# Attention and feed-forward on one core: the output of each head scaled and added on VectorE in place of ScalarE and GpSimd

## The reference

```
xn  = layernorm(x)                       # x: 2048 x 256
q,k,v = projections of xn                # 16 heads of width 128
p   = softmax(causal_mask(k q) / sqrt(128))
out = sum over heads of (p v) W_O        # 2048 x 256
y   = x + out + W2 . fwht(silu(W1 xn) * (W3 xn))
```

## Time and profile before

| | |
|---|---|
| median of 3 runs | 1452.96 us (1447.12 to 1454.21) |
| the profiled execution, its own time | 1451.85 us |
| its span, first to last instruction | 1450.0 us |
| granted TensorE clock, mean | 0.98 |
| attention stage, 16 periods | from about 286 us to about 1410 us |
| GpSimd's adds L369 | 128 of 1293 ns, 165.4 us in all |
| ScalarE's scalings L570 | 256 of 490 ns, 109.4 us in all |

### The profile page before, as it was taken

One profiled execution on the slowest core, in us unless ns is written; L12 is line 12 of the kernel. 1 busy time (PEld: TensorE's weight loads), 2 busy tenths in 40 slices (PEclk: granted clock), 3 DMA queues, 4 the chain that ended last, 5 costly groups with the idle time before them and its releaser, 6 DMA issues.

```text
span 1450.0 us, 26628 instructions
## 1 busy us (share of the span) xinstructions
PE 1351.6 (93%) x8104; PEld 1195.5 (82%) x8104; DVE 957.7 (66%) x2133; ACT 931.0 (64%) x1879; POOL 996.1 (69%) x660
## 2 busy tenths in 40 slices
PE   3989999969999999999999999999999999999985
PEld 2778888758888888888888888888888888888875
DVE  7743300277777777777777777777777767777760
ACT  3312244457777777777777777777777777777772
POOL 4420000066979797979797979797979787979785
PEclk8999999989999999999999999999999999999998
DMA  4100056579898989898988898888888888888884
GB/s 147 69 1 0 0 145 186 169 228 286 248 281 259 288 256 286 270 286 253 285 263 280 259 289 268 284 259 280 255 281 270 265 275 266 284 269 288 248 266 153
DMA packets 278459, 335.14 MB, mean 231 GB/s; under 512 B 62736, under 2 KB 251280, under 8 KB 273808
## 3 DMA queue, kind: packets, MB, share of 16 engines
q1 hardware_dynamic: 278416, 334.65, 73.6%
HBM read 173.08 MB, written 161.48 MB: 231 GB/s over the span
## 4 chain that ended last, share of the span: by engine, by line
PE 36%; POOL 23%; issue 20%; DVE 7%; ACT 5%; DMA 4%; SPq 3%; POOLq 0%; DVEq 0%; ACTq 0%
POOL pt_lo L378 15%; PE ps L827 12%; PE ps L828 12%; PE ps L829 12%; POOL acc L369 5%; SPq L276 3%; DMA scratch<-raw 3%; ACT raw L546 2%; DVE had L759 2%; DVE raw L769 2%; POOL v_lo L383 1%; DVE k_lo L672 1%; ACT pt_hi L555 1%; DMA raw<-w3t 1%; DMA pt_lo<-scratch 1%
## 5 line engine op out<-in xcount | busy, mean ns | idle before, releaser
L378 POOL TENSOR_TENSOR pt_lo<-pt_lo,pt_hi 128x640 fp32r<-128x640 f32 (+11 forms) x384 | 661.8, 1753 | 161.2 <-ACT pt_hi L555 161.1
L546 ACT ACTIVATE raw<-ps,had 128x1024 f32<-128x1024 f32 (+7 forms) x384 | 329.5, 867 | 226.0 <-DVE had L762 206.5
L769 DVE STREAM_TRANSPOSE raw<-raw 128x2048 f32<-128x2048 f32 (+15 forms) x256 | 322.0, 1292 | 99.5 <-ACT raw L546 97.2
L827 PE MATMUL ps<-pt_hi,v_hi 128*128 128x256 f32 (+1 forms) x1152 | 326.8, 284 | 29.7 <-POOL pt_lo L378 29.2
L828 PE MATMUL ps<-pt_lo,v_hi 128*128 128x256 f32 (+1 forms) x1152 | 331.7, 288 | 0.0
L829 PE MATMUL ps<-pt_hi,v_lo 128*128 128x256 f32 (+1 forms) x1152 | 329.8, 286 | 0.0
L555 ACT CAST pt_hi<-pt_lo 128x640 fp32r<-128x640 f32 (+11 forms) x384 | 283.4, 819 | 15.1 <-DMA pt_lo<-scratch 14.9
L759 DVE TENSOR_REDUCE had<-ps 128x1 f32<-128x1024 f32 (+1 forms) x256 | 238.0, 950 | 64.7 <-PE ps L829 64.5
L827 PEld LDWEIGHTS ps<-pt_hi,v_hi 128*128 128x128 f32 x1152 | 222.2, 193 | 38.6 <-issue 30.1
L827 PE MATMUL ps<-k_hi,q_hi 128*128 128x512 f32 (+3 forms) x640 | 239.0, 373 | 7.4 <-ACT raw L546 7.4
L829 PE MATMUL ps<-k_hi,q_lo 128*128 128x512 f32 (+3 forms) x640 | 234.6, 366 | 0.0
(11 more groups left out here) (102 smaller groups left out, 2218.3 us busy)
## 6 DMA issues: line engine op xcount, KB each, us to landing
all_values<-raw SPq DMA_DIRECT2D x16, 1024.0 KB, 5.0
v_next<-all_values SPq DMA_DIRECT2D x16, 1024.0 KB, 5.4
scratch<-raw SPq DMA_DIRECT2D x64, 256.0 KB, 5.5
pt_lo<-scratch SPq DMA_DIRECT2D x16, 1024.0 KB, 5.4
scratch<-raw SPq DMA_DIRECT2D x64, 240.0 KB, 5.0
pt_lo<-scratch SPq DMA_DIRECT2D x16, 960.0 KB, 6.0
scratch<-raw SPq DMA_DIRECT2D x64, 224.0 KB, 5.2
pt_lo<-scratch SPq DMA_DIRECT2D x16, 896.0 KB, 4.8
```

Of the source, the lines that this page charges most:

```text
L378: pool.tensor_tensor(lo, lo.bitcast(F32), hi.bitcast(F32), ALU.subtract).then_inc(pt_lo_done, 1)
L546: act.activation(to[:, first // P:(first + n) // P], ps[:, a * BANK:a * BANK + n].rearrange("p (i g k) -> p i g k", g=4, k=BLK), ACT.Exp, ...
L769: dve.transpose(v, v).then_inc(blocked, 1)
L827: pe.matmul(dst, a[0], b[0], start=start, stop=False, skip_group_check=True)
```

## The change

`output` moves from ScalarE to VectorE, where it is one SCALAR_TENSOR_TENSOR for each 128 queries: ring bank times `row_rcp` plus `acc`, written to `acc`. GpSimd's `add` and the two `share` buffers go. VectorE's new `output` stands in every step, behind `z_to_lo` of the small chunk and ahead of `maxima`; in step s it takes the chunk whose product TensorE made in step s-1. The ring bank is now free when VectorE has added it.

```diff
@@ gpsimd
-            def add(h, z):
-                c = Z_ORDER[z]
-                pool.wait_ge(shared, z_count(h, z))
-                pool.tensor_tensor(acc[:, 2 * c:2 * c + 2, :], share[:, z % 2, :, :],
-                                   acc[:, 2 * c:2 * c + 2, :], ALU.add).then_inc(out_added, 1)
...
-                        if not (first and back) and not (over and not back):
-                            add(h + back, z)
@@ scalar
-            def output(h, z):
-                c = Z_ORDER[z]
-                act.wait_ge(rcp_done, z_count(h, z))
-                wait(act, out_added, z_count(h, z) - 2)
-                act.wait_ge(wo_product, z_count(h, z))
-                for t in range(2):
-                    j = 2 * c + t
-                    ins = act.activation(share[:, z % 2, t, :], ring_bank(("O", z))[:, t * D:(t + 1) * D], ACT.Copy,
-                                         scale=row_rcp[:, j:j + 1])
-                ins.then_inc(shared, 1)
...
@@ vector
+            def output(h, z):
+
+                c = Z_ORDER[z]
+                dve.wait_ge(rcp_done, z_count(h, z))
+                dve.wait_ge(wo_product, z_count(h, z))
+
+                wait(dve, out_added, z_count(h, z) - 1)
+                for t in range(2):
+                    j = 2 * c + t
+                    ins = dve.scalar_tensor_tensor(
+                        out=acc[:, j, :], in0=ring_bank(("O", z))[:, t * D:(t + 1) * D], scalar=row_rcp[:, j:j + 1],
+                        in1=acc[:, j, :], op0=ALU.mult, op1=ALU.add)
+                ins.then_inc(out_added, 1)
...
-                for s in range(5 if over else STEPS):
+                for s in range(6 if over else STEPS):
                     if s in O_SMALL and not absent(O_SMALL[s][0]):
                         z_to_lo(h + O_SMALL[s][0], O_SMALL[s][1])
+
+                    back, z = (O_SMALL if s % 2 else O_BIG)[(s - 1) % STEPS]
+                    if s == 0:
+                        back -= 1
+                    if not absent(back):
+                        output(h + back, z)
                     if not over:
                         maxima(h, s, 0)
                         maxima(h, s, 1)
@@ tensor, ring_wait
-                    pe.wait_ge(shared, z_count(h - back - (1 if i >= 3 else 0), i))
+                    pe.wait_ge(out_added, z_count(h - back - (1 if i >= 3 else 0), i))
```

More of the change, by code:

```diff
@@ L127, in attention_ffn_kernel @@
         aux = sb("aux", [P, 4 * BANK], F32)
-        share = aux[:, 0:2 * BANK].rearrange("p (b t d) -> p b t d", b=2, t=2)
         mask = aux[:, 2 * BANK:3 * BANK]
@@ L212, in attention_ffn_kernel @@
         wo_product, rcp_done, summed = sem("wo_product"), sem("rcp_done"), sem("summed")
-        shared, out_added = sem("shared"), sem("out_added")
+        out_added = sem("out_added")
         G_FREE = 2
@@ L407, in period @@
                             p_to_lo(hh, ss, n)
[L408 to L411, removed]
             pool.wait_ge(wv_loaded, 16)
@@ L580, in period @@
                         z_to_hi(h + O_SMALL[s][0], O_SMALL[s][1])
[L581 to L586, removed]
                     if s in (1, 3) and not absent(O_BIG[s][0]):
@@ L600, in period @@
                         exponential(h, s, 2)
-                    if s in O_SMALL and not absent(O_SMALL[s][0]):
-                        output(h + O_SMALL[s][0], O_SMALL[s][1])
                     if s < 2 and not over:
```

## The result

The changed kernel takes 1469.97 us (median of 6 runs, 1468.4 to 1471.34), the kernel before 1452.28 us beside it; the ratio is 1.0129 (95% interval 1.0109 to 1.0149). It is 17.7 us slower; the forecast was 1471 us. Its profiled execution took 1468.4 us with a span of 1466.5 us, 16.5 us more than before.

What follows compares the result with a forecast made beforehand. TensorE bounds the kernel, busy for 93% of the span; only its waits count. 15 periods at 1.33 us add 20.0, the end saves 1.4: +18.6 on 1451.85 gives 1470.4, about 1471 us with the median; range 1447 to 1487 us.

Steps and rivals of the forecast that it cites:

- Rival A: Faster: outputs hide in VectorE's idle third, GpSimd's relief gives back 1.30 us in each of 15 periods; 1432 us, chance 0.13.
- step 4 of the walk: TensorE's sum of z = 0: GpSimd's relief gives back 0.42 of the 1.30 us wait; sum 1.33 us late.
- Rival B: Absorbed: ScalarE, relieved, hands z and p over earlier; at most 0.5 us late a period, about 1456 us, chance 0.16.
- step 0: Output of z = 2 on VectorE: 0.59 us hidden in the wait for scores, 0.09 us left.
- step 1: Output of z = 3 makes maxima 0.77 us late; 0.38 hidden, exponential 0.39 late, TensorE about 0.4 ahead of z = 4.
- the scores of step 3: TensorE waits about 0.7 us for ScalarE's exponential of step 2, 1.07 us late; the scores had 0.05 to spare.
- for z = 6: TensorE's product in step 3 waits 1.4 us or more for VectorE's low part of z; maxima ahead is 1.75 late.
- ahead of z = 0: TensorE's wait before the sum in step 4 shrinks from 1.30 to about 0.9 us.
- The chain to z = 0: GpSimd, its list full before, now waits for ScalarE's high part of v, 1.75 us late; VectorE, ScalarE, GpSimd chain.
- steps 5 to 7: VectorE's waits of 1.55 and 1.80 us hide the outputs; lateness against TensorE returns to nearly nothing, 1.33 us added once.
- p: VectorE's price of one output, two instructions of 0.34 us: 0.68 us, bounds 0.46 and 0.98.
- the walk's formulas: Lateness as a function of the price of an output p: 4p - 0.97 at step 3, 4p - 1.39 for the period.

Runs made afterwards that it cites:

- experiment 1: Changed kernel, same VectorE outputs moved behind maxima or z_to_lo, except z = 2 and z = 0: 1444.85 us, ratio 0.9969 to the kernel before.
- experiment 4: Kernel before without GpSimd's additions, ScalarE still scaling: 1446.05 us, ratio 0.9978.
- experiment 6: Kernel before without GpSimd's additions and with ScalarE's scaling cut to one column of one half: 1449.96 us, ratio 0.9983.
- experiment 7: Changed kernel with block 2 of v split in step 2 instead of step 3: 1458.32 us, ratio 1.0029 to the kernel before.
- experiment 8: Kernel before with block 2 of v split in step 2 instead of step 3: 1451.91 us, ratio 0.9996.
- experiment 3: Changed kernel with the second of each output's two instructions left out: 1450.33 us, ratio 1.0003 to the kernel before.
- experiment 5: Changed kernel with the output of z = 5 moved from step 3, ahead of maxima, to step 2, behind the reciprocals: 1458.06 us, ratio 1.0033.
- experiment 9: Kernel of experiment 1 with the low part of z = 6 moved ahead of the small row's maxima in step 3: 1458.25 us, ratio 1.0043.
- experiment 2: Kernel of experiment 1 with block 2 of v split in step 2 instead of step 3: 1446.66 us, ratio 0.9978.

## Why the prediction was right

**The direction and its cause were right.** The forecast blamed the place of the outputs in VectorE's list, not VectorE's busy share. Experiment 1 moves them with the same work and the loss turns into a small gain. Rival A, the relief of GpSimd, is real but worth 0.44 us a period and not 1.30 (experiment 4), as step 4 of the walk said: 0.42. Rival B needed ScalarE's relief to count; it gave nothing that could be seen (experiment 6), and the 1.72 us a period of the changed kernel is no half of the delays.

**Step by step.** In step 0 the cover was 0.59 us, and the wait of 0.51 us was used up. In step 1, 0.46 us of wait ahead of z = 4 where about 0.4 was named. Ahead of the scores of step 3, 0.68 us where 0.7 was named; for z = 6, 1.43 where at least 1.4 was; ahead of z = 0, 0.88 where 0.9 was. The third wait before, 0.28 us in step 2, was overlooked; it is gone, and gave back 0.14 us. The chain to z = 0 changed its releaser as described: GpSimd's 2.66 us for the high part of v shows it, and so does experiment 7, in which splitting v earlier removes that wait, while it does nothing before the change (experiment 8). Catching up in steps 5 to 7 was right too: all thirteen periods are alike (72.26 to 72.30 us).

**The term that was mis-sized is p.** I took 0.34 us an instruction from L773, whose shape is the same but which has no scalar from a tile. It is 0.39: p = 0.78 against 0.68. Put into the walk's formulas it gives 4 x 0.78 - 1.39 = 1.73 us a period; measured is 1.72 (72.30 - 70.58). It fits on the way there too: TensorE would be 0.59 us late in step 1, 1.32 at the scores of step 3 and 2.15 at z = 6, and its starts were 0.61, 1.35 and 2.12 late. The slope was checked from the other side as well: half outputs gave 70.90 us. One formula was stretched too far, at the low end: below p = 0.59 not all of the cover in step 0 is used, so p = 0.46 gives 3 x 0.46 - 0.38 - 0.42 = 0.58 us a period and not 0.45, and about 1460 us.

Of the overlap, each instruction of 0.469 us starts its successor after 0.39, the 0.08 us that the rows of before showed. The Trainium skill's sentence that the next operation waits for the empty pipe (VectorE: DVE Perf Modes, The DRAIN you can't avoid) does not describe these rows; the same section goes on that an operation that is not held starts earlier, which the prediction did not take in, and that agrees with them. The Trainium skill's fixed cost for a PSUM source does not fit: its section on the errata gives 120 + 256 cycles at 0.96 GHz, an estimate of 0.39 us for the instruction, where the trace has 0.469; that 0.39 us is also the distance from start to start is not explained by any run.

**Two errors cancelled.** That 1471 us was hit to 1 us is luck. With the right p the sum would have been 15 x 1.72 - 1.4 = 24.4 us, 1476 us on the profiled execution. The span grew by 16.5 us. The end gave what was expected: from the start of the last matmul to the end of the last addition it is 2.58 us before and 1.26 after. Between the first and the last wait ahead of z = 0 that both traces show (these rows are of the kernel before; those of the changed kernel stand above) it can be accounted for:

```profile
391.32 0.38 PE L827 MATMUL ps<-pt_hi,v_hi 128*128 128x256 f32 x1 [1.28 <-POOL pt_lo L378]
...
462.62 0.38 PE L827 MATMUL ps<-pt_hi,v_hi 128*128 128x256 f32 x1 [1.72 <-POOL pt_lo L378]
...
1312.97 0.38 PE L827 MATMUL ps<-pt_hi,v_hi 128*128 128x256 f32 x1 [1.27 <-POOL pt_lo L378]
```

Thirteen periods took 921.65 us before and 939.66 after: 18.0 us more, where 13 x 1.70 is 22.1. The 4.1 us are missing because thirteen times 70.58 is 917.5: the kernel before did not run at its own pace throughout. At 462.62 it waited 1.72 us. What held it up was not GpSimd's list this time but a late transfer of p, behind which the chain ran through ScalarE and GpSimd:

```profile
456.86 2.20 ACT L555 CAST pt_hi<-pt_lo 128x960 fp32r<-128x960 f32 x3 [1.44 <-DMA pt_lo<-scratch]
```

And behind the wait the clock fell:

```profile
462.00:464.00 2.00, 1.39 (x11) 1.39 (x12) 1.29 (x9) 2.00 (x5) 2.00 (x3) 1.00 0.97 354
464.00:466.00 2.00, 2.00 (x12) 2.00 (x11) 2.00 (x2) 2.00 (x6) 1.70 (x4) 0.52 1.07 375
466.00:468.00 2.00, 2.00 (x9) 1.82 (x9) 0.37 (x1) 2.00 (x4) 2.00 (x2) 0.63 0.88 241
468.00:470.00 2.00, 2.00 (x12) 1.73 (x12) 1.29 (x3) 0.46 (x2) 2.00 (x2) 1.00 0.50 130
```

It happened once more, at 1170 us, behind 1.75 us, with the transfer 1.29 us late. The two periods that end in these waits are 1.3 us longer than 70.58 together, the two behind them, with the low clock, 2.9 us. The changed kernel waits longer in sum, but no transfer of p is late in it, its longest wait in these periods is 1.46 us, and from 400 to 1350 us no stretch of 2 us of it has a granted clock below 0.95. So part of the loss was given back by late transfers and falls of the clock that no longer occur, which the forecast did not see. It is not a matter of the one profiled execution: the mean granted clock is 0.982 or 0.983 in all six executions of the changed kernel, and 0.980 on average (0.975 to 0.984) in the 79 of the kernel before that ran beside the experiments.

The two ends of the trace hold the rest. Ahead of the first row the changed kernel lost only 0.8 us where 1.7 was due: at 323 us, in the first period, it was still 0.97 us ahead, because TensorE was back at 2.4 GHz 2 to 3 us earlier than before, and from there to the first row it lost 1.74. Behind the last row it is 2.3 us shorter (134.75 against 137.03), where one more period and the end make 0.3 us more. Of these 2.6 us, 1.5 are again the clock, at the product of z = 6 in the last period; the wait and a window behind it, of before, then after:

```profile
1374.37 0.39 PE L827 MATMUL ps<-wo_hi,z_hi 128*128 128x256 f32 x1 [2.00 <-DVE z_lo L773]
...
1376.00:1378.00 2.00, 2.00 (x12) 2.00 (x11) 1.68 (x2) 1.11 (x2) 2.00 (x2) 0.50 1.02 368
...
1394.98 0.39 PE L811 MATMUL ps<-wo_hi,z_hi 128*128 128x256 f32 x1 [2.75 <-DVE z_lo L737]
...
1396.00:1398.00 2.00, 2.00 (x19) 2.00 (x18) 2.00 (x2) 2.00 (x5) 0.99 (x1) 1.00 0.74 201
```

The changed kernel came to this product 1.83 us later than before, and 4.5 us on only 0.35 us of that was left. The last 1.1 us are not traced to a cause. In the same way part of the 5.7 us by which experiment 3 undershot its expectation fits a clock that did not fall: its period came out as said, and it has no stretch of low clock from 400 to 1350 us, where the kernel before has two. Another 2.1 us is that the kernel before took 1449.73 us beside it and not the 1451.85 reckoned from. The miss of experiment 5 is of this second kind alone: the expected 11.7 us less than 1469.97 give 1458.3 us, measured were 1458.06, and the kernel before took 1453.33 us beside it, where 1452.28 had been the base.

## What to carry to other kernels

Busy shares did not tell what a move between engines would do; the place of the moved work in the receiving engine's list did. Ahead of the instruction that starts the longest chain, 0.78 us cost 0.78 us in each step whose slack was used up; behind it, in the same step, nothing that the periods show. And before counting a relief, look for what is late next at the same place: here v behind ScalarE's exponentials, and behind that a transfer, left 0.44 of 1.30 us.

## What the runs showed of the hardware beyond that

One long wait can cost more than two short ones. I looked at the granted clock of TensorE in stretches of 2 us from 400 to 1350 us in eleven executions. It fell to the lower of its two levels only beside waits of 1.69 us and more ahead of the sum of z = 0: at both waits of that length in the kernel before, in experiment 1 and in experiment 8, at all four in experiment 6 and at eleven of thirteen (1.71 to 1.81 us) in experiment 9. Mostly it was down for about 3.4 us, at a cost of about 1.4 us; twice, in experiments 6 and 9, for nearly 7 us. It did not fall at any wait of 1.60 us or less, of which the changed kernel and experiments 3, 4, 5 and 7 have nothing else. Length is not all of it: in experiment 2 it fell at one of four such waits only (1.71, 1.73, 1.77 and 1.71 us; at the second), and the rows don't tell what sets these apart. Nor does a longer wait make it certain: in the last period it fell behind the 2.00 us of the kernel before and not behind the 2.75 us of the changed kernel, both ahead of z = 6. Joining waits of 0.67 and 0.89 us into one of 1.78 us made the kernel 13 us slower (1458.25 us in experiment 9, 1444.85 us in experiment 1, each beside its own runs of the kernel before; by the ratios 1.0043 and 0.9969, 0.7%).

What made a wait that long was, but for experiment 9, a late transfer. In the kernel before and in experiments 1, 2, 6 and 8, ScalarE waited 1.12 us or more for step 1's p ahead of every one of these waits. In experiment 9 the order of VectorE's list did it, and the transfer was in time ahead of most.
